# Edge sum of a graph layer: gathered rows in high and low halves with three float32r products, and index fields packed into one

## What is computed

```
xn  = layernorm(x)
gnn = segment_sum(edge_weight[:, None] * xn[dst], src, 6250) + node_vec1
x   = x + gnn + mix(xn)          # linear attention over all rows, ends in a 256x256 matrix
out = x + ffn(layernorm(x))      # 8 experts, 2 of them for each row
```

## Time and profile before

| what | us |
|---|---|
| three timed runs | 2329.21, 2327.5, 2320.77 (median 2327.5) |
| the profiled execution | 2324.71 |
| its span, first to last instruction | 2322.8 |
| mean granted TensorE clock | 0.967 |
| TensorE matmuls busy in the span | 92% |
| VectorE | 88% |
| GpSimd | 71% |
| ScalarE | 52% |
| DMA traffic, mean | 102 GB/s |

### The profile page before, as it was taken

The page is one execution under the profiler, slowest core; times in us unless marked ns, Lnnn a source line. Parts: engine busy times, 40 slices in busy tenths (PEclk is TensorE's granted clock), DMA queues, the critical chain, the costliest instruction groups (busy, mean ns, idle before and its releaser), DMA issues. The chain is left out here.

```text
span 2322.8 us, 45681 instructions
## 1 busy us (share of the span) xinstructions
PE 2139.4 (92%) x16549; PEld 1879.9 (81%) x16550; DVE 2041.2 (88%) x3324; ACT 1215.4 (52%) x1688; POOL 1638.6 (71%) x1364
## 2 busy tenths in 40 slices
PE   7997799999999999999999999999999449999993
PEld 4665678888888888888888888888899449898892
DVE  7988999999999999999999999999788677666662
ACT  2336755555555555555555555554232257666561
POOL 3770067777777777777777777777777338888873
PEclk9997999999999999999999999999999679999997
DMA  4542433333333333333333333233555634544455
GB/s 139 158 114 73 127 114 92 89 90 101 92 91 100 88 92 92 101 89 89 92 101 92 91 99 91 90 90 91 141 152 155 199 60 74 76 76 75 75 74 137
DMA packets 160928, 235.85 MB, mean 102 GB/s; under 512 B 54834, under 2 KB 121805, under 8 KB 160490
## 3 DMA queue, kind: packets, MB, share of 16 engines
q0 software_dynamic: 70896, 164.43, 28.4%
q1 hardware_dynamic: 75536, 55.29, 8.6%
q10 hardware_dynamic: 14314, 13.68, 1.7%
HBM read 186.46 MB, written 53.24 MB: 103 GB/s over the span
## 5 line engine op out<-in xcount | busy, mean ns | idle before, releaser
L810 POOL DMA_INDIRECT picked<-xn_dram,place x1029 | 1185.8, 1152 | 445.7 <-issue 299.5
L908 PE MATMUL bank<-picked,pick_w 128*128 128x256 f32 x2058 | 501.4, 380 | 2.7 <-DMA picked<-xn_dram,place 2.7
L1020 ACT COPY stage<-bank 128x512 f32<-128x512 f32 x343 | 201.3, 587 | 496.5 <-PE bank L896 485.1
L908 PEld LDWEIGHTS bank<-picked,pick_w 128*128 128x128 f32 x2058 | 391.5, 190 | 56.4 <-DVE pick_w L1269 3.0
L974 ACT COPY field_rep<-fields 128x1666 bf16<-128x1666 bf16 (+1 forms) x235 | 398.4, 1718 | 0.8 <-DVE vals L1151 0.8
L904 PE MATMUL bank<-window,stage 128*128 128x256 f32 x1568 | 381.4, 386 | 0.0
L1262 DVE TENSOR_TENSOR hot_w<-hots,cur 128x1536 bf16<-128x1536 bf16 x343 | 328.5, 958 | 11.9
L904 PEld LDWEIGHTS bank<-window,stage 128*128 128x128 f32 x1568 | 282.6, 190 | 30.5 <-ACT stage L1020 0.2
L1258 DVE TENSOR_TENSOR hots<-iota_j,cur 128x1408 bf16<-128x1408 bf16 x343 | 302.6, 882 | 0.0
L896 PE MATMUL bank<-hot_w,hots 128*128 128x128 bf16 x4116 | 285.4, 219 | 1.5 <-DVE hot_w L1262 1.4
L904 PE MATMUL bank<-stage 128*128 128x256 f32 x1176 | 286.0, 386 | 0.0
(11 more groups left out here) (247 smaller groups left out, 3388.1 us busy)
## 6 DMA issues: line engine op xcount, KB each, us to landing
picked<-xn_dram,place POOLq DMA_INDIRECT x1029
xn_dram<-xn ACTq DMA_DIRECT2D x49, 128.0 KB, 1.9
xT_dram<-xT ACTq DMA_DIRECT2D x49, 128.0 KB, 2.2
base_dram<-acc SPq DMA_DIRECT2D x7, 896.0 KB
sum_dram<-acc SPq DMA_DIRECT2D x7, 896.0 KB
z_dram<-vals SPq DMA_DIRECT2D x7, 896.0 KB, 9.0
out_dram<-sum_dram SPq DMA_DIRECT2D x1, 6250.0 KB, 22.4
acc<-in_x_dram SPq DMA_DIRECT2D x6, 896.0 KB, 6.8
```

The lines of the kernel that those rows point to most:

```text
L810: pool.indirect_dma_start(out=picked[:, i % SETS * PICK + q, :], out_offset=None, in_=xn_dram, in_offset=bass.IndirectOffsetOnAxis(ap=plac ...
L908: mm = pe.matmul(sum_ps[pp], pick_w[i % SETS][:, q, :], picked[:, i % SETS * PICK + q, :], start=False, stop=(q == PICK - 1))
L1020: act.copy(block_sb[pp].rearrange("p j c -> p (j c)"), banks[pp][:, :]).then_inc(a_copied, 1)
```

## The change

The rows that are gathered lie in DRAM as two float32r halves (a rounded high part, and the rest), 2 KB for a row, and so does the one-hot weight of the picks; high x high, high x low and low x high are added. VectorE makes the high weighted one-hots, ScalarE the low ones. Place in `src` and place in `dst` become one bf16 field, taken apart again by bit operations after the sort. The buffers of one-hots and gathered rows go from 4 sets to 3.

```diff
-FIELDS = 5
-SRC, DST, W = 0, 1, 2
+FIELDS = 4
+END, W = 0, 1
+LOWEST = 32
# front, ScalarE: one more copy and one more store for a tile; `places` is gone
                 act.dma_start(xn_dram[t * P:(t + 1) * P, :], xn[t % DEPTH][:, :]).then_inc(stored[t % DEPTH], 16)
+                act.copy(xh[t % DEPTH][:, 0, :], xn[t % DEPTH][:, :]).then_inc(high_done, 1)
...
+                if t > 0:
+                    store_parts(t - 1)
+            def store_parts(t):
+                act.wait_ge(low_done, t + 1)
+                act.dma_start(xh_dram[t * P:(t + 1) * P, :], xh[t % DEPTH][:, :, :].rearrange("p k d -> p (k d)").bitcast(F32)).then_inc(stored[t % DEPTH], 16)
-            def places(c):
-                at = slice(c * UN, (c + 1) * UN)
-                act.wait_ge(cut, 4 * c + 2)
-                act.copy(fields[:, DST, at, :], dst_r[:, :, :]).then_inc(placed, 1)
-                act.wait_ge(cut, 4 * c + 4)
-                act.copy(fields[:, SRC, at, :], src_r[:, :, :]).then_inc(placed, 1)
# front, VectorE
+            def low_part(t):
+                dve.wait_ge(high_done, t + 1)
+                dve.tensor_tensor(xh[t % DEPTH][:, 1, :], xn[t % DEPTH][:, :], xh[t % DEPTH][:, 0, :].bitcast(F32), ALU.subtract).then_inc(low_done, 1)
...
+                elif m == 5:
+                    dve.wait_ge(cut, 4 * c + 4)
+                    dve.scalar_tensor_tensor(out=fields[:, END, at, :].bitcast(U16), in0=dst_r[:, :, :], scalar=float(LOWEST * P), in1=src_r[:, :, :],
+                                             op0=ALU.add, op1=ALU.add).then_inc(kept, 1)
...
                     normalize(t + DEPTH)
                     shift(t + DEPTH)
+                if t + DEPTH - 1 < NT:
+                    low_part(t + DEPTH - 1)
# edge_sum, GpSimd
-                used = t - SETS if i >= SETS else t - BU + SETS if i < BU - SETS else t - BU
-                if used >= 0:
-                    pool.wait_ge(o_done, used + 3)
+                if t >= SETS:
+                    pool.wait_ge(o_done, t - SETS + 3)
                 for q in range(PICK):
-                    pool.indirect_dma_start(out=picked[:, i % SETS * PICK + q, :], out_offset=None, in_=xn_dram,
+                    pool.indirect_dma_start(out=picked_f[:, t % SETS * PICK + q, :], out_offset=None, in_=xh_dram,
# edge_sum, TensorE `rows`
+                pe.wait_ge(pick_low, t + 1)
                 for q in range(PICK):
-                    mm = pe.matmul(sum_ps[pp], pick_w[i % SETS][:, q, :], picked[:, i % SETS * PICK + q, :], start=False, stop=(q == PICK - 1))
+                    high, low = (picked[:, t % SETS * PICK + q, m * D:(m + 1) * D] for m in range(2))
+                    pe.matmul(sum_ps[pp], pick_h[t % SETS][:, q, :], high, start=False, stop=False)
+                    pe.matmul(sum_ps[pp], pick_h[t % SETS][:, q, :], low, start=False, stop=False)
+                    mm = pe.matmul(sum_ps[pp], pick_l[t % 2][:, q, :], high, start=False, stop=(q == PICK - 1))
# edge_sum, ScalarE, called right behind each `evacuate`
+            def picks(t):
+                g, b = divmod(t, NT)
+                act.wait_ge(hot_done, t + 1)
+                if t >= 2:
+                    act.wait_ge(o_done, t + 1)
+                for q in range(PICK):
+                    ins = act.activation(pick_l[t % 2][:, q, :], hot[t % SETS][:, q, :], ACT.Copy, scale=weight_l[g % 2][:, b, q:q + 1])
+                ins.then_inc(pick_low, 1)
# edge_sum, VectorE
+            for f in range(HOTS):
+                if PICK <= f < AT_SRC:
+                    dve.tensor_scalar(ends[:, f, :].bitcast(U16), iota[:, :], float(P), float(LOWEST * P), ALU.mult, ALU.add)
+                else:
+                    dve.tensor_scalar(ends[:, f, :], iota[:, :], 1.0 / P, 1.0, ALU.mult, ALU.add)
+            def part(s, j, par):
+                dve.wait_ge(unpacked, s + 1)
+                bits = table[par][:, :, :].bitcast(U16)
+                both, dst = (bits[:, :, at:at + DENSE][:, :, bass.ds(j, 1)].rearrange("p b a -> p (a b)") for at in (AT_SRC, PICK))
+                dve.tensor_scalar(dst, both, 0x7F80, None, ALU.bitwise_and)
+                dve.tensor_scalar(both, both, P - 1, 0x3F80, ALU.bitwise_and, ALU.bitwise_or).then_inc(parted, 1)
# make_list: seven instructions, three of them behind a wait for the one ahead
+                dve.tensor_scalar(col, col, P - 1, 0x3F80, ALU.bitwise_and, ALU.bitwise_or)
+                dve.tensor_scalar(row[:, :], raw[:, END, :].bitcast(I32), 23, None, ALU.logical_shift_right).then_inc(listed, 1)
                 dve.tensor_tensor(pair[:, :], raw[:, W, :], raw[:, W + 1, :], ALU.add).then_inc(listed, 1)
+                dve.wait_ge(listed, LISTED * n + 2)
                 dve.tensor_tensor(place[par][:, bass.ds(q, 1), :].rearrange("p a b -> p (a b)"), row[:, :],
                                   first_row[:, bass.ds(s, 1)].broadcast_to([P, NB]), ALU.add)
+                dve.tensor_tensor(full[:, :], pair[:, :], raw[:, W + 2, :], ALU.add).then_inc(listed, 1)
+                dve.wait_ge(listed, LISTED * n + 3)
+                dve.tensor_copy(high, full[:, :]).then_inc(listed, 1)
+                dve.wait_ge(listed, LISTED * n + 4)
+                dve.tensor_tensor(low, full[:, :], high.bitcast(F32), ALU.subtract).then_inc(listed, 1)
# hots: the same shapes, `ends` in place of `iota_j`, and other waits
-                if free is not None:
-                    dve.wait_ge(a_done, free)
+                if t >= SETS:
+                    dve.wait_ge(a_done, t)
+                    dve.wait_ge(pick_low, t - SETS + 1)
```

More of the change, by code:

```diff
@@ L215, in front @@
         xn = [sb(f"xn{i}", [P, D]) for i in range(DEPTH)]
+        xh = [sb(f"xh{i}", [P, 2, D], F32R) for i in range(DEPTH)]
         xT = [sb(f"xT{i}", [P, 2, P]) for i in range(DEPTH)]
@@ L383, in _ @@
                     repeat_sample(t)
-                for k in range(NC):
-                    if t - APART[k] == 4:
-                        places(k)
+            store_parts(LAST)
         @block.tensor
@@ L606, in _ @@
                 shift(t)
+            for t in range(DEPTH - 1):
+                low_part(t)
             for t in range(NT):
@@ L651, in edge_sum @@
         slot = sb("slot", [P, CH, P], BF16)
-        vals_all = sb("vals", [P, CH * FIELDS * NB], BF16)
-        vals = vals_all[:, :].rearrange("p (c f b) -> p c f b", c=CH, f=FIELDS)
+        vals_all = sb("vals", [P, max(CH * FIELDS * NB, 2 * BU * D * 2)], BF16)
+        vals = vals_all[:, 0:CH * FIELDS * NB].rearrange("p (c f b) -> p c f b", c=CH, f=FIELDS)
         table = [sb(f"table{i}", [P, NB, ROWS], BF16) for i in range(2)]
-        raw = sb("raw", [P, FIELDS - 1, NB])
+        raw = sb("raw", [P, FIELDS, NB])
+        row = sb("row", [P, NB], I32)
+        ends = sb("ends", [P, HOTS, P], BF16)
         pair = sb("pair", [P, NB])
@@ L658, in edge_sum @@
         place = [sb(f"place{i}", [P, PICK, NB], I32) for i in range(2)]
-        weight = [sb(f"weights{i}", [P, NB, PICK]) for i in range(2)]
+        full = sb("full", [P, NB])
+        weight_h = [sb(f"weight_h{i}", [P, NB, PICK], F32R) for i in range(2)]
+        weight_l = [sb(f"weight_l{i}", [P, NB, PICK]) for i in range(2)]
         cur = [sb(f"cur{i}", [P, BU, ROWS, REP], BF16) for i in range(2)]
+        hot = [sb(f"hots{i}", [P, HOTS, P], BF16) for i in range(SETS)]
         cur_w = [sb(f"cur_w{i}", [P, BU, PICK, REP]) for i in range(2)]
-        hot = [sb(f"hots{i}", [P, HOTS, P], BF16) for i in range(SETS)]
-        pick_w = [sb(f"pick_w{i}", [P, PICK, P]) for i in range(SETS)]
-        picked = sb("picked", [P, SETS * PICK, D])
+        pick_h = [sb(f"pick_h{i}", [P, PICK, P], F32R) for i in range(SETS)]
+        pick_l = [sb(f"pick_l{i}", [P, PICK, P], F32R) for i in range(2)]
+        picked = sb("picked", [P, SETS * PICK, 2 * D], F32R)
+        picked_f = picked[:, :, :].bitcast(F32)
         stage = sb("stage", [P, 2 * DENSE * D])
@@ L715, in edge_sum @@
         o_done = sem("o_done"); o_added = sem("o_added")
-        listed = sem("listed"); pick_done = sem("pick_done"); rows_in = [sem(f"rows_in{i}") for i in range(SETS)]
+        listed = sem("listed"); pick_done = sem("pick_done"); pick_low = sem("pick_low"); rows_in = [sem(f"rows_in{i}") for i in range(SETS)]
         block = ctx.enter_context(nc.Block())
@@ L889, in sort, with blocks @@
                         mix((s - 1) * BU + i)
-            def blocks(t, buf, pp):
+            def blocks(t, pp):
+                buf = t % SETS
                 pe.wait_ge(w_done, t + 2)
@@ L895, in blocks, with rows @@
                     for part in range(3):
-                        mm = pe.matmul(block_ps(pp, j), hot[buf][:, PICK + DENSE + j, :], hot_w[buf][:, part, j, :],
+                        mm = pe.matmul(block_ps(pp, j), hot[buf][:, PICK + j, :], hot_w[buf][:, part, j, :],
                                        start=(part == 0), stop=(part == 2))
                 mm.then_inc(a_done, 1)
```

(16 more changed lines are left out.)

129 lines of the change are left out of this document (69 added, 60 removed).

## The result

The changed kernel took **2339.0 us** (median of 7 runs, 2332.2 to 2350.1) against 2326.0 for the kernel before (7 runs): a ratio of 1.0064, 95% interval 1.0042 to 1.0086. It is slower by about 13 us, where the forecast was 2321.5 us, 6 less than the 2327.5 of the kernel before. The range held the time; the direction was wrong.

The account below looks back on a forecast made before the run. TensorE, VectorE and GpSimd were taken to bound the long middle within 0.2 us of each other per unit. Terms -10 - 3 - 2 + 9 = -6 us against the median of 2327.5 gave 2321.5, range 2288 to 2372.

Parts of the forecast that it names:

- the front: Stretch from about 20 to 180 us, before sorting and mixing: VectorE's added subtractions cost 4.5 to 19 us, taken as +9.
- they are awaited two iterations later: Front: the 49 extra stores of 256 KB are waited for only two iterations on; no time was charged for them.
- if the front grows by 20 us: Sign named beforehand that the forecast is wrong; the front was expected to become some 9 us longer.
- still under what the 16 engines can do: Front: extra stores add about 84 GB/s to 145, DMA share 0.54 to 0.85, which the DMA engines can still carry.
- The middle: The 42 units that mostly sort and sum: 30.5 us each in place of 30.73, GpSimd setting the pace; -10 us.
- VectorE's 30.57: VectorE's time per unit before the change, averaged from 30.36 without a list and 30.84 with one; forecast afterwards 30.05.
- The gathers' mean: GpSimd's time per gather in a unit: 1.154 us before, a little less afterwards through fewer collisions with VectorE; unit 30.5.
- Rival S: GpSimd's gathers get dearer, any addition counting 1029 times: 2353 us, or 2527 if row length counts; chance 0.31.
- The last units: Last 7 units, 30.46 us each before: TensorE loses 1.5 but GpSimd's 21 gathers still want about 30; -3 us.
- Sorting beside the mixing: Windows sorted beside the mixing products, 179 to 306 us, VectorE full: fewer `vals`, more small operations; together -2 us.
- low one-hot: ScalarE's three 128x128 activations per block, 0.29 us each, 6.1 per unit; hidden by 8 us of slack.
- Picks and table on TensorE: TensorE per unit: picks 1.30 to 1.08 us a block, table 3.65 to 2.92; unit about 28.5, no longer the bound.

## Why the prediction was wrong

*The step that failed* is the front: "So it costs between 4.5 (all idle time used) and 19 (none); I take +9." The bounds were made from VectorE's work only. That part was fair, if 6 too small: +14.9 measured alone, inside the bounds, with 0.42 us for a subtraction where 0.33 was read from the add. The second part, the wait of `normalize` for the new stores, was costed at nothing, with "they are awaited two iterations later" as its cover, and the cover did not hold: the store stands one iteration back in ScalarE's queue and lands 2.1 to 6.6 us after its issue, and two iterations of 3.1 us are too little for both. That is +15.5, alone; on top of the work it is +14.2 (29.1 less 14.9). Profiles of the same front in six kernels give 176.0 to 182.2 us, so +28 to +34 in place of +9: some 20 us, more than the whole error of the total (17.5 against the median). The prediction did name the sign: "if the front grows by 20 us" the forecast is wrong. It also named `normalize` as what would be late next, but gave that no price and no rival, and "still under what the 16 engines can do" judged the stores by bandwidth, where their delay mattered.

*The middle was right.* Unit 30.5 forecast, 30.31 measured; -15.4 us in 42 units against -10 (17.2 won in the 41 that sort, 1.7 lost in the one that doesn't). The reason was right too: with a third of the gathers gone the unit is VectorE's 30.10 (30.05 forecast), with VectorE relieved by 4 us it stays GpSimd's, 30.4. The gathers' mean was 1.141 where it was put "a little under" 1.154. Two things in it were luck. VectorE's 30.57 was the length of two early units; in the trace of before the later units with a list take 31.2, the 41 average 30.73, and these are lengths of units in which TensorE was busy all the time, not VectorE's own demand. And the mean of the gathers hangs on how they fall: with 1 KB rows the same unit took 30.67. The Trainium skill (SBUF — State Buffer, "Who interferes with whom") infers that `tensor_tensor` does not hold up descriptor generation. No profile here agrees with it: in after 662 of the 663 gathers that start more than 0.04 us into such a product, and 0.125 or more before its end, end 0.80 to 0.85 us after it, and the other 13 profiles show the same with 1 to 7 exceptions each.

*Rival S's price was right, its mechanism not.* "Whatever is added, times 1029": the run with 1 KB rows shows 0.02 us of mean worth 16 us in 42 units. But the length of the rows, which it feared, costs nothing; only the meetings do.

*The last units* were forecast at -3 and came out at +7.9 in the profiled execution. In other profiles with the same last units (a ring of four, GpSimd's low halves) they took 191.5 and 185.8 us, and with the short `hot_w` 180.3, against 185.6 to 186.5 in four kernels with the last units of before. So the loss is nothing or a few us, from stalls of TensorE on late gathers that differ from one execution to the next, and the +7.9 is in part the chance of one execution. The gain of TensorE's shorter picks is mostly lost there: with two gathers of three the six units took 174.3, so what keeps them longer is the gathers. What makes the long stalls is open. The DMA engines were full in the one that is shown, and with small stores no unit was long in one profile; but the 180.3 had the long stores too.

*Sorting beside the mixing*: -2 forecast, -2.1 measured. *ScalarE*: 0.396 us for a low one-hot where 0.22 to 0.37 was the bound, and it did not matter, as argued (899 of 1243 us busy). *Picks and table on TensorE*: as forecast (from start to start, a block 3.53 us and the table 2.91), and hidden by GpSimd and VectorE.

## What to carry to other kernels

A store added to a ring has two prices: its work on the engines, and the time from the last write of the slot to the landing of its store, which is the place of the issue in a queue plus 2.1 to 6.6 us here. Compare the second with the time from that last write to the next write of the slot, before anything is called awaited later. That is not the ring's depth times the iteration: here it was under two iterations of 3.1 us for a ring of three, since the last write comes an iteration after the first. Where three engines are within 1% of each other, work taken from two of them is worth what the third leaves, here 15 us in the middle for 66 us of TensorE's busy time in all.

## What the runs showed of the hardware

A gather of 128 rows takes GpSimd 0.94 us with rows of 1 KB or 2 KB, and 0.305 before it, unless it starts within one of VectorE's products of two SBUF inputs: then it ends 0.82 us after that product. A gather that starts in the first 0.035 us of such a product escapes (all 43 of after take under 0.97 us). VectorE's add with one input in PSUM (0.945 us on average in the 164 gathers of after that start beside it), idle time, or a product that starts after the gather leave it at 0.95 too. And a kernel with less to transfer (1 KB rows) or less to compute (a third of `hot_w`) can be slower or no faster, since the meetings of the two engines fall differently: with 1 KB rows 16 us of the kernel's time went with that.
